# One forward transform in place of two for values and weights in an attention-plus-FFN kernel, with the values' second form made by DMA

## The chip, the core and the metric

The kernel is one program on one core of a Trainium2 chip. The metric is the device time of one execution in microseconds; the number to predict is the median over runs of the changed kernel. The core has five engines that take part here: TensorE (PE in the profile, its weight loads are PEld), VectorE (DVE), ScalarE (ACT), GpSimd (POOL), and SyncE (SP), whose queue issues every DMA of this program. Each engine carries out its own instructions in order, and semaphores tie the engines together.

## The reference, cut to what matters

Sixteen batches of 64 tokens with 512 channels go through two residual blocks. The first is an autocorrelation attention between the normalised x and a context, for every channel on its own; the second is a gated FFN of width 1792 in float16 weights.

```python
# block 1: q = layernorm(x), k = v = ctx, every channel alone, length L = 64
corr = ifft(fft(q) * conj(fft(k))).real
w, idx = top_k(corr, 8)
w = softmax(w)
out = sum over i of w[i] * v[min(idx[i] + pos, L - 1)]
x = x + tanh(g_xattn) * out
# block 2
h = silu(layernorm(x) @ W_gate.T) * (layernorm(x) @ W_up.T)
x = x + tanh(g_ffn) * (h @ W_down.T)
```

## The kernel before, in words

Two batches make a pair (128 partitions), and there are eight pairs, 0 to 7. Fourier transforms are matmuls with constant matrices. Keys, queries, values and weights are transformed with a contraction of 64 rows (one batch), 128 output rows and 512 channels.

For pairs 1 to 7 every float32 operand is split into a float16 high and a float16 low part (steps named `..._hi` on ScalarE and `..._lo` on GpSimd). One transform of a pair is then six matmuls of 64x512 (three products of parts for each of two batches; helper `transform`, L785). A batch's rows are partitions 0 to 63 or 64 to 127, so the two batches use different row halves of the array. Pair 0 is not split and runs in float32 (`transform32`, L793).

The gather with a clamped index is done as a correlation over twice the length, so that values and weights are needed at the even and at the odd frequencies of length 128. Per pair the steps are these:

- `kspec` transforms the context at even frequencies, `kcopy` (two ACT copies, L563) takes the result out of PSUM into `kv_spec`; `vspec` transforms the context at odd frequencies, `vcopy` (two ACT copies, L569) takes that out; `qspec` transforms the queries. All three use PSUM banks 4 and 5, so each waits for the copies of the one before.
- `prod` (DVE, L663) multiplies queries with keys, `p_hi` and `p_lo` split it, `lags` (24 small matmuls, L866 to L868) transforms back to correlations over lags.
- The softmax over the best eight: `max` (L673), `sub` (L681 for all lags and L683 for the best eight), `match` (L696), `exp` (ACT, L585 and L586), `sum` (DVE: the sum L702, the mask L704, the reciprocal L706), `scale` (GpSimd L503; for pair 0 on DVE, L710).
- `w_rows_hi`, `w_rows_lo` split the weights, `w_t` (two transposing DMAs, L450) turns them; for pair 0 `wt` does it on TensorE.
- `wspec:p` transforms the weights at even frequencies, `mix_prod:p` and `mix_prod:p.1` (DVE, L727) multiply by the even spectra; `wspec:p.1` transforms them at odd frequencies into the same PSUM banks 6 and 7, and `mix_prod:p.2`, `:p.3` multiply by the odd spectra. `m_hi` and `m_lo` split the products, `mix` (12 matmuls, L918) transforms back.
- `residual` (DVE, L745, with the statistics L640, L642) adds to x; `rstd2` (GpSimd), `xn`, `x_rows_hi` (ACT), `x_rows_lo` (GpSimd, L522) and `x_t` (two transposing DMAs, L460) make the FFN's input.
- The FFN runs in four parts per pair: `gate`, `up` (L802, 128 or 64 columns a matmul), `tanh` (ACT, L624), `silu` (DVE, L764), `hid` (DVE, L772), `h_hi` (ACT, L631), `h_lo` (GpSimd, L527), `down` (L967), then `out` and `store`.

The order of all steps is written out by hand in one list, `ORDER`. Each engine walks the list and carries out its own part of each step, so the list fixes every engine's order, SP's too. `kspec` of a pair waits until `match` and `sub` of the pair before are done, since banks 4 and 5 hold the correlations too. The attention of later pairs is laid between the FFN parts of earlier ones. `mixed` and `kv_spec` have two buffers each. `WARM_UP` gives the number of matmuls on zeroed data at three places of pair 0 (L815): at the start, before `kspec:1` and before `wt:0`.

Of the kernel before, what the change touches and what calls it, by code (L numbers as in the profile page):

```python
# [112 lines left out]
warm:0 stats1:0 rstd1:0 kspec:0 q_norm:0 qspec:0 kcopy:0 kcopy:0.1 vspec:0 prod:0 stats1:1 k_hi:1 lags:0  # L113
vcopy:0 prod:0.1 rstd1:1 vcopy:0.1 max:0 lags:0.1 warm:0.1 sub:0 k_lo:1 q_norm:1 match:0 exp:0 kspec:1
warm:0.2 q_hi:1 sum:0 q_lo:1 scale:0 kcopy:1 max:0.1 wt:0 kcopy:1.1 sub:0.1 w_hi:0 vspec:1 match:0.1 gates:0
wspec:0 exp:0.1 scales:0 vcopy:1 sum:0.1 wspec:0.1 vcopy:1.1 mix_prod:0 qspec:1 scale:0.1 mix_prod:0.2 wt:0.1
mix:0 prod:1 stats1:2 p_hi:1 mix:0.1 w_hi:0.1 p_lo:1 prod:1.1 wspec:0.2 residual:0 p_hi:1.1 k_hi:2 p_lo:1.1
wspec:0.3 mix_prod:0.1 rstd2:0 lags:1 mix_prod:0.3 max:1 rstd1:2 xn:0 xt:0 sub:1 k_lo:2 mix:0.2 q_norm:2
x_hi:0 match:1 mix:0.3 k_hi:3 q_hi:2 k_lo:3 x_lo:0 exp:1 kspec:2 residual:0.1 q_lo:2 gate:0 kcopy:2 sum:1
rstd2:0.1 up:0 tanh:0 scale:1 kcopy:2.1 silu:0 xn:0.1 vspec:2 w_rows_hi:1 hid:0 gate:0.1 w_t:1 w_rows_lo:1  # L120
stats1:3 vcopy:2 vcopy:2.1 rstd1:3 h_hi:0 qspec:2 xt:0.1 prod:2 h_lo:0 up:0.1 x_hi:0.1 w_t:1.1 p_hi:2 x_lo:0.1
prod:2.1 tanh:0.1 p_lo:2 gate:0.2 stats1:4 p_hi:2.1 q_norm:3 p_lo:2.1 silu:0.1 hid:0.1 wspec:1 rstd1:4
h_hi:0.1 lags:2 mix_prod:1 up:0.2 mix_prod:1.1 m_hi:1 h_lo:0.1 max:2 k_hi:4 m_lo:1 q_hi:3 wspec:1.1 sub:2
m_hi:1.1 gate:0.3 m_lo:1.1 mix_prod:1.2 exp:2 match:2 tanh:0.2 q_lo:3 mix:1 m_hi:1.2 tanh:0.3 m_lo:1.2 sum:2
kspec:3 up:0.3 mix_prod:1.3 kcopy:3 scale:2 silu:0.2 m_hi:1.3 hid:0.2 kcopy:3.1 m_lo:1.3 mix:1.1 w_rows_hi:2
silu:0.3 vspec:3 h_hi:0.2 hid:0.3 w_t:2 w_rows_lo:2 mix:1.2 vcopy:3 residual:1 vcopy:3.1 h_lo:0.2 h_hi:0.3
qspec:3 down:0 rstd2:1 prod:3 w_t:2.1 prod:3.1 p_hi:3 h_lo:0.3 xn:1 down:0.1 x_rows_hi:1 p_lo:3 p_hi:3.1 x_t:1
p_lo:3.1 wspec:2 mix_prod:2 x_rows_lo:1 lags:3 mix_prod:2.1 m_hi:2 down:0.2 max:3 q_norm:4 m_lo:2 x_t:1.1
m_hi:2.1 down:0.3 sub:3 k_lo:4 match:3 exp:3 wspec:2.1 m_lo:2.1 q_hi:4 gate:1 sum:3 mix_prod:2.2 scale:3
kspec:4 mix_prod:2.3 m_hi:2.2 up:1 out:0 m_hi:2.3 m_lo:2.2 w_rows_hi:3 tanh:1 m_lo:2.3 w_t:3 gate:1.1 kcopy:4  # L130
silu:1 kcopy:4.1 w_rows_lo:3 stats1:5 mix:2 hid:1 q_lo:4 mix:2.1 mix:2.2 w_t:3.1 h_hi:1 vspec:4 residual:2
h_lo:1 up:1.1 vcopy:4 vcopy:4.1 rstd2:2 tanh:1.1 qspec:4 k_hi:5 silu:1.1 wspec:3 prod:4 gate:1.2 prod:4.1
p_hi:4 mix_prod:3 p_hi:4.1 p_lo:4 mix_prod:3.1 up:1.2 tanh:1.2 p_lo:4.1 hid:1.1 xn:2 silu:1.2 x_rows_hi:2
k_lo:5 gate:1.3 hid:1.2 h_hi:1.1 x_t:2 lags:4 h_hi:1.2 h_lo:1.1 down:1 tanh:1.3 max:4 m_hi:3 h_lo:1.2 match:4
up:1.3 x_rows_lo:2 down:1.1 rstd1:5 sub:4 x_t:2.1 silu:1.3 exp:4 wspec:3.1 hid:1.3 h_hi:1.3 kspec:5
mix_prod:3.2 q_norm:5 h_lo:1.3 down:1.2 sum:4 kcopy:5 m_lo:3 kcopy:5.1 mix_prod:3.3 m_hi:3.1 scale:4 gate:2
m_lo:3.1 w_rows_hi:4 m_hi:3.2 w_t:4 down:1.3 w_rows_lo:4 tanh:2 up:2 m_hi:3.3 out:1 m_lo:3.2 silu:2 gate:2.1
m_lo:3.3 w_t:4.1 hid:2 stats1:6 h_hi:2 q_hi:5 mix:3 mix:3.1 q_lo:5 mix:3.2 vspec:5 residual:3 h_lo:2 up:2.1
vcopy:5 rstd1:6 vcopy:5.1 tanh:2.1 qspec:5 rstd2:3 wspec:4 prod:5 gate:2.2 silu:2.1 p_hi:5 prod:5.1 p_lo:5
hid:2.1 p_hi:5.1 up:2.2 tanh:2.2 p_lo:5.1 h_hi:2.1 silu:2.2 xn:3 h_lo:2.1 gate:2.3 hid:2.2 x_rows_hi:3 lags:5  # L140
mix_prod:4 x_t:3 tanh:2.3 h_hi:2.2 silu:2.3 up:2.3 mix_prod:4.1 m_hi:4 h_lo:2.2 down:2 hid:2.3 k_hi:6 max:5
m_hi:4.1 k_lo:6 h_hi:2.3 down:2.1 match:5 q_norm:6 x_rows_lo:3 k_hi:7 h_lo:2.3 sub:5 x_t:3.1 down:2.2 m_lo:4
exp:5 m_lo:4.1 wspec:4.1 q_hi:6 kspec:6 mix_prod:4.2 down:2.3 mix_prod:4.3 m_hi:4.2 sum:5 kcopy:6 gate:3
m_lo:4.2 kcopy:6.1 out:2 m_hi:4.3 scale:5 up:3 tanh:3 m_lo:4.3 w_rows_hi:5 silu:3 w_t:5 gate:3.1 w_rows_lo:5
q_lo:6 mix:4 tanh:3.1 mix:4.1 w_t:5.1 silu:3.1 mix:4.2 vspec:6 residual:4 up:3.1 vcopy:6 vcopy:6.1 hid:3
rstd2:4 qspec:6 wspec:5 prod:6 gate:3.2 mix_prod:5 p_hi:6 prod:6.1 xn:4 p_lo:6 mix_prod:5.1 p_hi:6.1 up:3.2
hid:3.1 tanh:3.2 p_lo:6.1 x_rows_hi:4 silu:3.2 h_hi:3 x_t:4 wspec:5.1 h_hi:3.1 h_lo:3 gate:3.3 mix_prod:5.2
x_rows_lo:4 lags:6 hid:3.2 tanh:3.3 m_hi:5 up:3.3 silu:3.3 h_lo:3.1 x_t:4.1 m_hi:5.1 down:3 store:0 h_hi:3.2
m_lo:5 hid:3.3 m_hi:5.2 mix_prod:5.3 down:3.1 max:6 h_lo:3.2 m_hi:5.3 h_hi:3.3 sub:6 h_lo:3.3 gate:4 k_lo:7
match:6 m_lo:5.1 down:3.2 tanh:4 exp:6 m_lo:5.2 up:4 sum:6 m_lo:5.3 stats1:7 scale:6 down:3.3 silu:4 kspec:7  # L150
rstd1:7 out:3 mix:5 hid:4 kcopy:7 mix:5.1 kcopy:7.1 mix:5.2 w_rows_hi:6 vspec:7 residual:5 h_hi:4 w_t:6
gate:4.1 q_norm:7 rstd2:5 up:4.1 tanh:4.1 w_rows_lo:6 vcopy:7 silu:4.1 xn:5 gate:4.2 w_t:6.1 vcopy:7.1 hid:4.1
store:1 q_hi:7 x_rows_hi:5 q_lo:7 up:4.2 tanh:4.2 x_t:5 h_hi:4.1 store:2 silu:4.2 h_lo:4 qspec:7 h_lo:4.1
hid:4.2 wspec:6 prod:7 h_hi:4.2 x_rows_lo:5 gate:4.3 mix_prod:6 p_hi:7 prod:7.1 down:4 m_hi:6 h_lo:4.2 x_t:5.1
mix_prod:6.1 store:3 m_hi:6.1 p_lo:7 up:4.3 p_hi:7.1 tanh:4.3 p_lo:7.1 wspec:6.1 silu:4.3 down:4.1
mix_prod:6.2 m_lo:6 hid:4.3 m_hi:6.2 mix_prod:6.3 h_hi:4.3 m_lo:6.1 lags:7 m_hi:6.3 down:4.2 max:7 h_lo:4.3
m_lo:6.2 match:7 gate:5 m_lo:6.3 sub:7 down:4.3 tanh:5 exp:7 up:5 out:4 sum:7 mix:6 silu:5 scale:7 mix:6.1
hid:5 mix:6.2 gate:5.1 w_rows_hi:7 residual:6 w_t:7 w_rows_lo:7 up:5.1 rstd2:6 tanh:5.1 silu:5.1 xn:6 w_t:7.1
gate:5.2 hid:5.1 x_rows_hi:6 h_hi:5 x_t:6 store:4 h_hi:5.1 h_lo:5 up:5.2 tanh:5.2 silu:5.2 x_rows_lo:6 wspec:7
hid:5.2 h_lo:5.1 x_t:6.1 gate:5.3 mix_prod:7 up:5.3 tanh:5.3 h_hi:5.2 silu:5.3 down:5 mix_prod:7.1 m_hi:7  # L160
m_hi:7.1 m_lo:7 wspec:7.1 h_lo:5.2 down:5.1 mix_prod:7.2 hid:5.3 m_hi:7.2 mix_prod:7.3 gate:6 m_hi:7.3
h_hi:5.3 h_lo:5.3 down:5.2 m_lo:7.1 tanh:6 silu:6 m_lo:7.2 up:6 m_lo:7.3 down:5.3 mix:7 out:5 mix:7.1 mix:7.2
hid:6 gate:6.1 residual:7 h_hi:6 h_lo:6 up:6.1 tanh:6.1 rstd2:7 silu:6.1 xn:7 gate:6.2 hid:6.1 up:6.2 tanh:6.2
x_rows_hi:7 silu:6.2 h_hi:6.1 x_t:7 gate:6.3 hid:6.2 h_lo:6.1 up:6.3 h_hi:6.2 x_rows_lo:7 tanh:6.3 down:6
silu:6.3 hid:6.3 h_lo:6.2 x_t:7.1 h_hi:6.3 store:5 down:6.1 h_lo:6.3 down:6.2 gate:7 down:6.3 tanh:7 up:7
silu:7 out:6 store:6 gate:7.1 hid:7 up:7.1 tanh:7.1 h_hi:7 silu:7.1 h_lo:7 gate:7.2 hid:7.1 up:7.2 tanh:7.2
h_hi:7.1 silu:7.2 h_lo:7.1 gate:7.3 hid:7.2 up:7.3 h_hi:7.2 tanh:7.3 h_lo:7.2 down:7 silu:7.3 hid:7.3 h_hi:7.3
# [20 lines left out]
def on_vector(step, p, n):  # L190
# [809 lines left out]
```

## Time and profile before

| | |
|---|---|
| median of 3 runs | 225.96 us (225.72 to 226.12) |
| the profiled execution's own time | 226.68 us |
| its span, first to last instruction | 224.8 us |
| mean granted TensorE clock | 0.991 of full |
| PE busy | 215.2 us, 96% |
| DVE, POOL, ACT busy | 138.3, 137.7, 111.0 us |

The span is 1.88 us shorter than the profiled execution's own time, and that execution is 0.72 us above the median of the runs. Busy times are of one execution. A matmul's own length in the trace (381 ns for 512 columns) contains the pipeline's fill, so that neighbours overlap; what a group of matmuls costs is read from the chain of work or from the distance between starts.

### The profile page before, as it was taken

To read this page: it belongs to the slowest core of one execution; us is meant where nothing else is said; L and a number is where in the kernel's file an instruction comes from. 1 tells how busy PE (TensorE), PEld (TensorE's weight loads), DVE (VectorE), ACT (ScalarE), POOL (GpSimd) and SP (SyncE) were. 2 spreads that over 40 slices of the span, in tenths; PEclk is the share of its full clock that TensorE was granted. 3 is DMA by queue.
4 is the path that set the end of the run, shared out by engine and by line. 5 is a ranking of instruction groups with operands and counts; after the bars stand their busy time and mean duration, and the time that the engine had idled before them with its cause. 6 is when DMAs were issued, how large, how long until landed. Compare 5 with 4: busy or idle time off the path is not lost.

```text
span 224.8 us, 6753 instructions
## 1 busy us (share of the span) xinstructions
PE 215.2 (96%) x2779; PEld 148.4 (66%) x2779; DVE 138.3 (61%) x407; ACT 111.0 (49%) x208; POOL 137.7 (61%) x165
## 2 busy tenths in 40 slices
...
GB/s 152 335 434 425 388 140 50 4 3 47 47 4 51 0 50 0 50 3 23 28 25 26 23 73 3 23 143 70 4 26 93 26 0 3 25 73 50 0 3 47
DMA packets 19918, 16.69 MB, mean 74 GB/s; under 512 B 15920, under 2 KB 16304, under 8 KB 19504
## 3 DMA queue, kind: packets, MB, share of 16 engines
...
## 4 chain that ended last, share of the span: by engine, by line
PE 86%; DVE 6%; DMA 2%; issue 2%; POOL 1%; ACT 1%; SPq 0%; DVEq 0%; ACTq 0%
PE psum L802 44%; PE psum L967 20%; PE psum L785 10%; PE psum L918 4%; PE psum L903 2%; DMA ctx_sb<-ctx 2%; DVE probs L696 1%; DVE raw_stats L640 1%; PE psum L793 1%; PE psum L885 1%; PE psum L866 1%; ACT xn L537 1%; DVE x_sb L745 1%; PE psum L867 1%; PE psum L868 1%
## 5 line engine op out<-in xcount | busy, mean ns | idle before, releaser
L802 PE MATMUL psum<-xt_hi,wg 128*128 128x128 f16 (+1 forms) x504 | 54.0, 213 | 0.0
L802 PE MATMUL psum<-xt_hi,wu 128*128 128x128 f16 (+1 forms) x504 | 53.9, 213 | 0.0
L802 PE MATMUL psum<-xt_lo,wg 128*128 128x128 f16 (+1 forms) x504 | 53.9, 213 | 0.0
L802 PE MATMUL psum<-xt_lo,wu 128*128 128x128 f16 (+1 forms) x504 | 53.8, 213 | 0.0
L527 POOL TENSOR_TENSOR hid_lo<-hid,hid_hi 128x512 f16<-128x512 f32 (+2 forms) x32 | 33.0, 1037 | 29.0 <-ACT hid_hi L631 29.0
L802 PEld LDWEIGHTS psum<-xt_hi,wg 128*128 128x128 f16 x504 | 44.8, 98 | 6.2 <-issue 5.5
L802 PEld LDWEIGHTS psum<-xt_hi,wu 128*128 128x128 f16 x504 | 44.9, 98 | 3.0 <-issue 2.1
L802 PEld LDWEIGHTS psum<-xt_lo,wu 128*128 128x128 f16 x504 | 45.0, 98 | 0.8
L802 PEld LDWEIGHTS psum<-xt_lo,wg 128*128 128x128 f16 x504 | 45.1, 98 | 0.7
L967 PE MATMUL psum<-wd,hid_hi 128*128 128x512 f16 x112 | 42.5, 379 | 0.1
L967 PE MATMUL psum<-wd,hid_lo 128*128 128x512 f16 x112 | 42.4, 379 | 0.0
L764 DVE SCALAR_TENSOR_TENSOR act<-act,psum 128x512 f32<-128x512 f32 (+2 forms) x32 | 19.7, 616 | 32.7 <-ACT act L624 32.4
L513 POOL TENSOR_TENSOR mixed_lo<-mixed,mixed_hi 128x512 f16<-128x512 f32 x28 | 32.6, 1177 | 4.4 <-ACT mixed_hi L602 4.4
L624 ACT ACTIVATE act<-psum 128x512 f32<-128x512 f32 (+2 forms) x32 | 17.2, 539 | 35.2 <-PE psum L802 35.2
L727 DVE SCALAR_TENSOR_TENSOR mixed<-psum,kv_spec 128x512 f32<-128x512 f32 x32 | 21.3, 680 | 10.0 <-PE psum L785 10.0
L631 ACT ACTIVATE hid_hi<-hid 128x512 f16<-128x512 f32 (+2 forms) x32 | 18.0, 570 | 14.8 <-DVE hid L772 14.7
L772 DVE TENSOR_TENSOR hid<-act,psum 128x512 f32<-128x512 f32 (+2 forms) x32 | 19.8, 618 | 8.4 <-PE psum L802 5.9
L498 POOL TENSOR_TENSOR prod_lo<-prod,prod_hi 128x512 f16<-128x512 f32 x14 | 16.1, 1158 | 11.3 <-ACT prod_hi L575 11.1
L602 ACT ACTIVATE mixed_hi<-mixed 128x512 f16<-128x512 f32 x28 | 17.4, 625 | 10.6 <-DVE mixed L727 10.5
L967 PEld LDWEIGHTS psum<-wd,hid_hi 128*128 128x128 f16 x112 | 11.0, 98 | 12.9 <-issue 1.8
L967 PEld LDWEIGHTS psum<-wd,hid_lo 128*128 128x128 f16 x112 | 11.0, 98 | 10.6
L663 DVE TENSOR_TENSOR prod<-psum,kv_spec 128x512 f32<-128x512 f32 x16 | 10.8, 685 | 8.7 <-PE psum L785 4.6
...
## 6 DMA issues: line engine op xcount, KB each, us to landing
out<-x_sb SPq DMA_DIRECT2D x8, 256.0 KB, 2.3
...
x_sb<-x SPq DMA_DIRECT2D x4, 256.0 KB, 5.2
ctx_sb<-ctx SPq DMA_DIRECT2D x4, 256.0 KB, 5.1
...
```

What stands on the lines that cost most here:

```text
L498: nc.gpsimd.tensor_tensor(prod_lo[:, e, n, :], prod[:, e, n, :], prod_hi[:, e, n, :], ALU.subtract).then_inc(split_sems["p_lo", False], 1)
L513: nc.gpsimd.tensor_tensor(mixed_lo[:, e, n, :], mixed[:, e, n, :], mixed_hi[:, e, n, :], ALU.subtract).then_inc(split_sems["m_lo", False], 1)
L527: nc.gpsimd.tensor_tensor(hid_lo[:, e, first:end, tok], hid32[:, n % 2, 0:ffn_cols(p, n)].rearrange("p (a t) -> p a t", a=end - first), hi ...
L602: nc.scalar.activation(mixed_hi[:, e, n, :], mixed[:, e, n, :], ACT.Copy).then_inc(mixed_high, 1)
L624: nc.scalar.activation(act32[:, n % 2, 0:cols], psum[:, gate_bank(p, n), 0:cols], ACT.Tanh, scale=0.5).then_inc(tanh_done, 1)
L631: nc.scalar.activation(hid_hi[:, e, first:end, tok], hid32[:, n % 2, 0:ffn_cols(p, n)].rearrange("p (a t) -> p a t", a=end - first), ACT.C ...
L727: nc.vector.scalar_tensor_tensor(mixed[:, e, n, :], psum[:, w_bank(p, m, b), :], MIX_UP, kv_spec[:, e, n, :], ALU.mult, ALU.mult).then_inc ...
L764: nc.vector.scalar_tensor_tensor(a, a, 1.0, psum[:, gate_bank(p, n), 0:cols], ALU.add, ALU.mult).then_inc(silu_done, 1)
L772: nc.vector.tensor_tensor(hid32[:, n % 2, 0:cols], act32[:, n % 2, 0:cols], psum[:, up_bank(p, n), 0:cols], ALU.mult).then_inc(hid_done, 1)
L785: last = nc.tensor.matmul(psum[:, banks[b], :], consts[rows(b), forward(name, part)], data[rows(b), :], start=data is high and part == 0, ...
L802: last = nc.tensor.matmul(psum[:, bank, a * n:(a + 1) * n], w[:, k, m * P:(m + 1) * P], xt[:, e, k, tok], start=(k == 0 and part == 0), st ...
L967: last = nc.tensor.matmul(psum[:, down_bank(p), :], hid[:, e, m, :], wd[:, m, :], start=(m == 0 and part == 0), stop=(m == MT - 1 and part ...
```

## The change

- For pairs 1 to 7 there is one transform of the context, with the matrix `values`: 64 columns of even frequencies and 64 of odd ones. Keys and values come out of the same result. `vspec` remains for pair 0 alone.
- `vcopy` of a pair is one ACT copy of 128 x 1024 (two banks); `kcopy` is two ACT copies of 64 x 1024, which write the even half into the upper and the lower 64 partitions of `k_spec`. `qspec` waits for all three.
- The values' second form (real and imaginary parts exchanged) is not transformed: the new step `turn` issues five DMAs on SP's queue, four from `v_spec` to `v_turned` in SBUF (31 or 32 partitions x 4 KB each) and one of two context rows (4 KB) from HBM.
- There is one transform of the weights per pair (matrix `weights`), and all four `mix_prod` follow it. The second pair of them waits for the five DMAs.
- `mixed` has one buffer in place of two, so `mix_prod` of a pair waits for `m_lo` of the pair before.
- The softmax's steps are cut finer: `sub` and `sub8`, `exp` and `exp8`, `total` (sum and reciprocal) and `mask`, each with its semaphore, with the same instructions.
- The two last loads (context and x of pairs 4 to 7, 1 MB each) are issued behind `turn:1` and no longer at the start.
- `WARM_UP` goes from ((12, 4), (3, 7), (2, 7)) to ((12, 4), (0, 7), (11, 7)), that is 12, 0 and 11 matmuls. `ORDER` is another list. Pair 0 keeps its float32 arithmetic.

```diff
-WARM_UP = ((12, 4), (3, 7), (2, 7))
+WARM_UP = ((12, 4), (0, 7), (11, 7))
...
-    kv_spec = sb("kv_spec", [P, 2, 4, D])
+    v_spec = sb("v_spec", [P, 2, 2, D])
+    v_turned = sb("v_turned", [P, 2, 2, D])
+    k_spec = sb("k_spec", [P, 2, 2, D])
...
-    mixed = sb("mixed", [P, 2, 4, D])
+    mixed = sb("mixed", [P, 4, D])
...
+                if step == "turn":
+                    sp.wait_ge(v_copied, copies(p))
+                    if p > 2:
+                        sp.wait_ge(mixed_done, 4 * p - 4)
+                    for to, first, count in ((1, 33, 31), (32, 0, 32), (64, 96, 32), (96, 64, 32)):
+                        sp.dma_start(v_turned[to:to + count, e, :, :], v_spec[first:first + count, e, :, :])\
+                          .then_inc(v_moved[e], 16)
+                    sp.dma_start(v_turned[0:1, e, :, :], last_rows[p:p + 1, :, :]).then_inc(v_moved[e], 16)
+                    if p == 1:
+                        load(ctx_sb, cv, 4, PAIRS, ctx_loaded[4])
+                        load(x_sb, xv, 4, PAIRS, x_loaded[4])
...
+                if step == "vcopy" and p > 0:
+                    act.wait_ge(k_spectra, p + 1)
...
+                    nc.scalar.activation(v_spec[:, e, :, :], psum[:, k_bank(p, 0):k_bank(p, 1) + 1, :], ACT.Copy,
                                          scale=SPEC).then_inc(v_copied, 1)
+                if step == "kcopy" and p > 0:
...
+                    nc.scalar.activation(k_spec[rows(n), e, :, :], psum[0:L, k_bank(p, 0):k_bank(p, 1) + 1, :], ACT.Copy,
+                                         scale=SPEC).then_inc(k_copied, 1)
...
+                if step == "mix_prod" and p > 0:
+                    m, b = n // 2, n % 2
+                    dve.wait_ge(w_spectra, nth("wspec", p))
+                    if m == 0:
+                        dve.wait_ge(v_copied, copies(p))
+                    else:
+                        dve.wait_ge(v_moved[e], nth_turned(p))
+                    if p == 1:
+                        dve.wait_ge(mix_done, last_of("residual", 0))
+                    else:
+                        dve.wait_ge(*split_count("m_lo", p - 1, n))
+                    nc.vector.scalar_tensor_tensor(mixed[:, n, :], psum[:, w_bank(p, m, b), :], MIX_UP,
+                                                   (v_spec, v_turned)[m][:, e, b, :], ALU.mult, ALU.mult)\
+                      .then_inc(mixed_done, 1)
...
-                        pe.wait_ge(k_copied, 2 * p + 2)
-                        last = transform(banks, "odd_v", k_hi[:, e, :], k_lo[:, e, :])
...
-                    transform([w_bank(p, n, b) for b in range(2)], ("even", "odd")[n], w_hi[:, e, :], w_lo[:, e, :])\
+                    transform([w_bank(p, 0, b) for b in range(2)], "weights", w_hi[:, e, :], w_lo[:, e, :])\
```

The parts of the new `ORDER` that the prediction speaks of (each "..." leaves steps out):

```
vcopy:0 prod:0.1 lags:0 ... max:0 sub:0 q_hi:1 kspec:1 warm:0.2 sub8:0
max:0.1 exp:0 q_lo:1 exp8:0 kcopy:1 match:0 total:0 vcopy:1 sub:0.1 mask:0 sub8:0.1 scale:0
...
mix:1.2 ... down:0 ... down:0.1 ... wspec:2 ... lags:3 ... down:0.2 max:3 k_lo:4 down:0.3
x_t:1.1 sub:3 match:3 exp:3 rstd1:5 q_norm:4 m_hi:2 sub8:3 kspec:4 mix_prod:2.1 exp8:3
m_lo:2 gate:1
...
q_lo:4 mix:2.1 vcopy:4 mix:2.2 w_rows_lo:3 up:1.1 h_hi:1 residual:2 k_hi:5 rstd1:6 w_t:3.1 tanh:1.1 qspec:4
rstd2:2 turn:3 gate:1.2 prod:4 prod:4.1 p_hi:4 silu:1.1 p_hi:4.1 p_lo:4 up:1.2 tanh:1.2 xn:2 h_lo:1 silu:1.2
hid:1.1 x_rows_hi:2 wspec:3 p_lo:4.1 h_hi:1.1 x_t:2 gate:1.3 mix_prod:3 x_rows_lo:2 hid:1.2 lags:4 tanh:1.3
```

## Rows read from the trace of the kernel before

**Rows 1.** Busy time by stage, us (and instructions): PE, PEld, DVE, ACT, POOL, clock, DMA.
```profile
0.00:30.30 30.30, 25.74 (x122) 10.42 (x123) 21.76 (x84) 15.76 (x31) 12.58 (x24) 0.94 0.92 345
30.30:62.60 32.30, 30.41 (x597) 20.25 (x596) 24.48 (x81) 21.77 (x41) 27.43 (x33) 1.00 0.14 29
62.60:215.00 152.40, 152.40 (x2031) 114.66 (x2030) 90.42 (x241) 72.52 (x135) 95.91 (x107) 1.00 0.16 33
```

**Rows 2.** Groups of PE's instructions: busy us, mean ns; the transforms of the context.
```profile
L785 PE MATMUL psum<-k_hi,consts 64*128 64x512 f16 x56 | 10.8, 381 | 0.7 <-DVE probs L696 0.5
```

**Rows 3.** Chain of work, 70 to 75 us: start, us, what.
```profile
70.35 0.75 PE psum L785 x6
...
73.00 1.40 PE psum L785 x12
```

**Rows 4.** PE in order of time: first matmuls of gate:1 and of gate:2.
```profile
62.55 0.23 PE L802 MATMUL psum<-xt_hi,wg 128*128 128x128 f16 x1
...
87.09 0.22 PE L802 MATMUL psum<-xt_hi,wg 128*128 128x128 f16 x1
```

**Rows 5.** PE in order of time: lags:3, with the idle time before it.
```profile
58.41 0.19 PE L866 MATMUL psum<-consts,prod_hi 128*128 128x64 f16 x1 [0.48 <-POOL prod_lo L498]
```

**Rows 6.** Chain of work, pair 0's first softmax half: start, us, what.
```profile
10.67 0.55 DVE top L673 x4
...
11.23 0.42 DVE expo L681
11.66 0.91 DVE expo L683
...
14.11 1.18 DVE probs L710
```

**Rows 7.** DVE in order of time: pair 0's second L683.
```profile
16.19 0.18 DVE L683 TENSOR_TENSOR expo<-top 128x32 f32<-128x32 f32 x1
```

**Rows 8.** Busy time by stage inside pair 0's work, the columns of group 1.
```profile
12.00:15.30 3.30, 1.90 (x11) 0.41 (x9) 3.16 (x14) 2.29 (x6) 1.79 (x2) 1.00 0.99 421
15.30:19.00 3.70, 3.66 (x20) 1.58 (x20) 3.67 (x22) 2.07 (x6) 0.00 (x0) 1.00 0.98 417
...
27.00:29.50 2.50, 2.50 (x6) 0.27 (x4) 2.16 (x18) 1.86 (x5) 1.91 (x3) 0.50 1.05 387
```

**Rows 9.** Groups of ACT's instructions, shapes apart: busy us, mean ns, idle before.
```profile
L569 ACT ACTIVATE kv_spec<-psum 128x512 f32<-128x512 f32 x16 | 8.8, 593 | 4.9 <-PE psum L785 4.7
...
L624 ACT ACTIVATE act<-psum 128x256 f32<-128x256 f32 x7 | 2.6, 374 | 4.5 <-PE psum L802 4.5
```

**Rows 10.** DMA issues: count, KB each, median us to landing.
```profile
out<-x_sb SPq DMA_DIRECT2D x8, 256.0 KB, 2.3
...
ctx_sb<-ctx SPq DMA_DIRECT2D x4, 256.0 KB, 5.1
...
xt_lo<-xn_lo SPq DMA_TRANSPOSE x7, 2.5
```

**Rows 11.** SP's queue in order of time: start, us to issue.
```profile
9.16 0.67 SPq L437 DMA_DIRECT2D wd<-w_down  x1
...
69.10 1.19 SPq L450 DMA_TRANSPOSE w_lo<-w_lo_rows  x1
78.32 1.19 SPq L460 DMA_TRANSPOSE xt_hi<-xn_hi  x1
82.30 1.19 SPq L460 DMA_TRANSPOSE xt_lo<-xn_lo  x1
```

**Rows 12.** POOL in order of time, from p_lo:4 to x_rows_lo:2.
```profile
75.23 2.29 POOL L498 TENSOR_TENSOR prod_lo<-prod,prod_hi 128x512 f16<-128x512 f32 x2 [1.81 <-ACT prod_hi L575]
77.47 1.16 POOL L490 TENSOR_TENSOR k_lo<-ctx_sb,k_hi 128x512 f16<-128x512 f32 x1
78.89 2.27 POOL L527 TENSOR_TENSOR hid_lo<-hid,hid_hi 128x512 f16<-128x512 f32 x2 [0.25 <-ACT hid_hi L631]
81.12 1.15 POOL L522 TENSOR_TENSOR xn_lo<-xn,xn_hi 128x512 f16<-128x512 f32 x1
```

More of the change, by code:

```diff
@@ L95, in parts @@
         return high, (m - high).astype(np.float16)
-    for n, m in enumerate((even_kv, even, odd_v, odd)):
+    for n, m in enumerate((query, values, weights)):
         for part, v in enumerate(parts(m)):
@@ L112 @@
 ORDER = """
[L113 to L167, printed above, removed]
@@ L168 @@
-h_lo:7.3 down:7.1 down:7.2 down:7.3 out:7 store:7
+warm:0 stats1:0 rstd1:0 kspec:0 q_norm:0 kcopy:0 qspec:0 kcopy:0.1 vspec:0 stats1:1 prod:0 k_hi:1 rstd1:1
+vcopy:0 prod:0.1 lags:0 vcopy:0.1 k_lo:1 lags:0.1 warm:0.1 q_norm:1 max:0 sub:0 q_hi:1 kspec:1 warm:0.2 sub8:0
+max:0.1 exp:0 q_lo:1 exp8:0 kcopy:1 match:0 total:0 vcopy:1 sub:0.1 mask:0 sub8:0.1 scale:0 kcopy:1.1 stats1:2
+wt:0 w_hi:0 qspec:1 match:0.1 rstd1:2 exp:0.1 wspec:0 gates:0 prod:1 exp8:0.1 prod:1.1 p_hi:1 wspec:0.1
+mix_prod:0 k_hi:2 p_lo:1 q_norm:2 mix_prod:0.2 mix:0 mask:0.1 p_hi:1.1 total:0.1 mix:0.1 q_hi:2 scale:0.1
@@ new lines @@
+p_lo:1.1 scales:0 residual:0 k_lo:2 lags:1 k_hi:3 wt:0.1 max:1 w_hi:0.1 rstd2:0 wspec:0.2 sub:1 q_lo:2 xn:0
+wspec:0.3 match:1 exp:1 k_lo:3 xt:0 mix_prod:0.1 kspec:2 sub8:1 mix:0.2 mix_prod:0.3 exp8:1 x_hi:0 mask:1
+kcopy:2 mix:0.3 turn:1 x_lo:0 total:1 vcopy:2 gate:0 residual:0.1 scale:1 kcopy:2.1 stats1:3 rstd2:0.1 qspec:2
+tanh:0 w_rows_hi:1 up:0 prod:2 w_t:1 w_rows_lo:1 prod:2.1 p_hi:2 silu:0 xn:0.1 p_lo:2 gate:0.1 p_hi:2.1
+stats1:4 p_lo:2.1 xt:0.1 w_t:1.1 hid:0 tanh:0.1 up:0.1 x_hi:0.1 silu:0.1 rstd1:3 h_hi:0 x_lo:0.1 turn:2 lags:2
```

223 lines of the change are left out of this document (146 added, 77 removed).

## The prediction

> **What bounds the kernel now.** I read the busy time by stage first. The reader is to see three stretches [rows 1]. From 62.6 us, where the FFN of pair 1 begins, to 215 us PE is busy for 152.40 of 152.40 us, while DVE has 90.4, POOL 95.9 and ACT 72.5 us of work: TensorE alone sets the time there, and a matmul less is time less. From 30.3 to 62.6 us PE has 30.41 of 32.30 us, but POOL has 27.43: two engines are nearly full. Up to 30.3 us (pair 0) PE has 25.74 us, DVE 21.76, and the chain of work runs over DVE's softmax [rows 6].
>
> Then I read what a transform costs. The group of PE's instructions gives a matmul 381 ns [rows 2]; six would be 2.3 us. That is the wrong number: it holds the pipeline's fill, and the two row halves run beside each other. The chain of work gives 0.75 us for six matmuls that stand alone and 1.40 us for twelve in a row [rows 3], so a transform is worth 0.75 us alone and 0.65 us where it stands beside another one.
>
> **The change part by part.**
>
> *Fewer transforms.* Seven `vspec` and seven second `wspec` go, 84 matmuls. Which of the fourteen lie in the full stretch follows from the order: `gate:1` began at 62.55 us [rows 4], and `vspec:4` to `vspec:7` and `wspec:3.1` to `wspec:7.1` stand behind it, nine. Two of them (`wspec:3.1`, `wspec:4.1`) stood beside a `kspec`: 7 x 0.75 + 2 x 0.65 = 6.55 us, call it 6.6. The other five (`vspec:1`, 2 and 3, `wspec:1.1`, `wspec:2.1`) would be 5 x 0.75 = 3.75 us if PE were the bound there too. `vspec:1` lies in pair 0's stretch, under DVE's softmax, and is worth nothing. The other four lie where POOL has 27.43 of 32.30 us; `lags:3` even waited 0.48 us for `p_lo` [rows 5]. And `kspec:4` moves from behind `gate:1` to before it. It needs `match:3`, which follows `lags:3`, `max` and `sub`: DVE's pieces of a whole pair are twice those of half a pair (0.55 and 0.42 us for `max` and `sub` [rows 6]), and only two parts of `down` and nothing else cover them, now that `wspec:2.1` is gone. So I take 1.7 of the 3.75 us, between 0 and 3.75.
>
> *Pair 0's order.* Before, `scale:0` came after one half's chain alone. Now `max:0.1`, `sub:0.1` and `sub8:0.1` stand ahead of it: 0.55 + 0.42 + 0.2 to 0.9 us [rows 6, 7], 1.2 to 1.9 us later for `wt:0`. The second half gains most of that back, since its pieces are done already, and `stats1:1` leaves the place between the two `prod`. Behind it, `mix_prod:0.1` and `mix_prod:0.3` now stand after `max:1`, `sub:1` and `match:1`. Net, I take 0.7 us lost up to the first `gate`; bounds 0 and 1.5. The eleven warming matmuls lie where PE waits for `scale:0` anyway: PE was busy 1.90 of 3.30 us from 12.0 to 15.3 us [rows 8]. From 27.0 to 29.5 us the granted clock was 0.50, that is 1.2 GHz, behind a time in which PE had waited [rows 8]. The new order leaves such waits in the same place, so I take that loss as it is; at full clock these 2.5 us would be some 1.25 us, a bound on the other side.
>
> *Copies on ACT.* Before, four copies of 512 columns per pair, 593 ns each; 256 columns take 374 ns [rows 9], so 1,024 columns come to 593 + 2 x 219 = 1.03 us. Three of them are 3.1 us a pair against 4 x 0.59 = 2.4 us, 0.7 us more, 5 us in all. ACT has 72.5 of 152.4 us in the full stretch [rows 1], which hides it. `qspec` waits for all three behind `kspec`; in the new order `mix`, parts of `down` and `up` or more stand between. Cost nothing; were the cover gone, up to 3.1 us a pair.
>
> *`turn` on DMA and on SP's queue.* The trace has no copy from SBUF to SBUF. The nearest rows are a 256 KB store in 2.3 us and a 256 KB load in 5.1 us [rows 10]; the four pieces are 128 KB each, so 2.3 to 5.1 us to land behind the last issue. An issue takes 0.67 us [rows 11], a transpose's 1.19; five are 3.4 to 6.0 us. So `v_turned` is there 6 to 11 us after `turn` begins. I take the lower end, since the DMA share in the full stretch is 0.16 [rows 1]. Who waits: `mix_prod:p.2`. For pair 3 it stands between `x_t:2` and `x_t:2.1` in the order, at 78.32 and 82.30 us before, and SP is free from 70.3 us [rows 11]: 8 to 12 us. What is queued behind it on SP: for pairs 3 to 5 the next `x_t`, for pair 6 `w_t:6.1`. SP stood idle from 69.10 + 1.19 to 78.32 us before `x_t:2` [rows 11], 8 us, which hides 3.4 to 6.0. Nothing, then.
>
> By a rule of the Trainium skill ("SBUF — State Buffer", Door 1: The DMA port swizzle) partitions 0 to 31 reach only eight of the sixteen DMA ports of SBUF, so each of these copies of 32 partitions would run at no more than half the rate of a full one. No row here shows it. By the rule the landing time would be the upper one, and the sum would stay as it is as long as that fits into the 8 to 12 us above.
>
> *Moved loads.* The last two loads are issued behind `turn:1`. In the rows the DMA share is full up to 29.5 us [rows 8] with the weights ahead of them, so the queue is still fed when they come, and `k_hi:4`, the first to need them, stands just before `lags:3`, which began at 58.41 us [rows 5]. Nothing.
>
> *One buffer of `mixed`, finer softmax.* `m_lo` of the pair before is a whole pair back: nothing. The finer steps are the same instructions. Their price depends on what stands beside them: L683 took 0.91 us with GpSimd at work and 0.18 us in a stretch in which GpSimd did nothing [rows 6 to 8]. This agrees with the Trainium skill ("SBUF — State Buffer", the part on the shared pair), by which a VectorE instruction with two SBUF inputs and a GpSimd instruction lock each other out. By that rule, with GpSimd denser after the change, the seven masks and seven `sub8` would take up to 0.7 us longer each, 10 us of DVE in all; DVE has 62 us of room in the full stretch, so the sum stays.
>
> *New waits in the full stretch.* The cover between the helpers' chain and the FFN shrinks. `x_t:2.1` was issued at 82.30 us and lands 2.5 us later [rows 10, 11], 84.8 us; `gate:2` began at 87.09 [rows 4]: 2.3 us of room, and two transforms (1.4 us) leave it. But `x_rows_lo:2` also moves: it stood behind two `p_lo`, one `k_lo` and two `h_lo` [rows 12], now behind two `p_lo` and one `h_lo`, two times 1.15 us earlier. I take 0.5 us for all pairs together; bounds 0 and 3.3 (half of 6.6).
>
> **Sum.** -6.6 - 1.7 + 0.7 + 0.5 = -7.1 us. The profiled execution's 226.68 us become 219.6; the median of the runs is 0.72 us below that execution, so 225.96 - 7.1 = 218.9 us.
>
> **The rivals.**
>
> *A, everything counts.* PE bounds the start too, and the stretch at half clock goes: 6.55 + 3.75 = 10.3 us, up to 11.5 with the clock: 214.5 to 215.7 us. For it: PE is 94% busy from 30.3 to 62.6 us, and the order is new as a whole. Against it: POOL's 27.43 us there [rows 1].
>
> *B, the helpers become the bound.* With 6.6 us less, POOL's 95.9 us lie in some 146 us, 66%, but the work comes in bursts, and `gate` of each pair waits for a chain with 2.3 us of room [rows 4, 11]. PE then waits 0.5 us or so in each of six pairs, and the start gives nothing: -6.6 + 0.7 + 3.3 = -2.6, 223.4 us; halfway from my forecast, 221.2. For it: the waits at 58.4 us [rows 5]. Against it: the chain of POOL's steps is shortened as well [rows 12].
>
> *C, SP's queue holds up `x_t` (slower).* SP is in order. If `turn` had to wait for something late, or an issue took as long as it takes to land, the five would hold the queue for 5 x 2.3 = 11.5 us. That is 3.5 us more than SP's idle time of 8 us; less the 2.3 us of room, `gate` comes 1.2 us late, and with the 5.1 us a piece of the slow row 5 x 5.1 - 8 - 2.3 = 15 us late. It decides from 10.3 us a `turn` on, and makes the kernel slower from about 1.5 us a pair over that for pairs 3 to 7. With 3 us for each of five pairs: -7.1 + 15 = +7.9, 233.9 us. Against it: these issues return in 0.67 to 1.19 us, their data land 2.3 to 5.1 us later [rows 10, 11].
>
> *D, no change.* Would need the same at about 1.4 us a pair; nothing in the rows speaks for it.
>
> **How the numbers follow.** My forecast, 0.62; A 0.12; B 0.20; C 0.04; D 0.02. The forecast's own range is 217.3 to 220.9: the start's term between 0 and 3.75 with the loss of pair 0 against it. The range for 8 in 10 goes to A's upper end, 215.6, and into B, 222.5. Under 0.2% (0.45 us) a measurement cannot tell from no change. Faster: forecast, A and B, 0.94; same 0.02; slower 0.04.
>
> **What the profile after would show.** PE's L785-like groups have 126 matmuls instead of 210, and PE's busy time is about 10 us less (1.3 us come back as warming matmuls). The full stretch has PE at 100% still, if B is wrong; waits for `x_t`'s DMAs before `gate` would show B or C. ACT's copies in pairs 1 to 7 sum to about 21 us. The five `turn` issues stand in SP's idle time; a wait of `mixed` for a DMA would make my reading of `turn` wrong. The first `gate` matmul starts at 30.3 to 31.8 us. Gate:1 starting before 61 us would mean that the start gave more than I allow; after 63.5 us, that it gave nothing.

## The result: 1.7% slower, and the profile after

The changed kernel takes 229.88 us (median of 4 runs, 228.90 to 231.27), the kernel before on the same chip 226.04 us (225.72 to 226.48). The ratio is 1.017, 95% interval 1.011 to 1.024. The forecast was 218.9 us, 11 us too low, with the wrong sign. The profiled execution took 230.77 us, with a span of 228.7 us.

Busy time by stage, the columns and stretches of [rows 1]:

```profile
0.00:30.30 30.30, 25.76 (x133) 10.94 (x134) 21.12 (x87) 19.70 (x33) 13.68 (x25) 0.94 0.90 314
30.30:62.60 32.30, 28.10 (x557) 20.82 (x554) 21.57 (x65) 17.82 (x30) 23.29 (x30) 0.89 0.55 84
62.60:215.00 152.40, 144.14 (x1915) 109.65 (x1914) 90.22 (x253) 77.13 (x134) 98.64 (x108) 1.00 0.35 51
```

In the stretch in which TensorE was busy for 152.40 of 152.40 us it now is for 144.14: 8.3 us of idle time have come into a stretch that had none. The DMA share has gone from 0.16 to 0.35 there. Seven `turn` of 0.52 MB are not much in bytes, so the share (the time that packets are in the engines) says that packets wait there. In the second stretch the clock is 0.89 in place of 1.00. The wait list of PE says for what it waited (us in total, times, longest):

```profile
PE psum L869 <- issue: 4.7, 2, 2.8
PE psum L886 <- issue: 2.6, 1, 2.6
PE psum L869 <- DVE probs L765: 1.8, 2, 1.2
PE psum L886 <- DMA xt_lo<-xn_lo: 1.7, 1, 1.7
```

L869 is `transform` (L785 before), L886 `gate` and `up` (L802 before). "Issue" is a wait for which the view names nobody. The two of L869 stand right before `wspec:4` and `wspec:6`, whose operands are brought by transposing DMAs; the one of 2.6 us of L886 lies before 40.2 us, at the start. These DMAs' median times from issue to landing stand beside it (before, `w_hi` took 2.5, `w_lo` 3.2, `xt_hi` 2.4 and `xt_lo` 2.5 us):

```profile
w_hi<-w_hi_rows SPq DMA_TRANSPOSE x7, 2.5
w_lo<-w_lo_rows SPq DMA_TRANSPOSE x7, 4.6
xt_hi<-xn_hi SPq DMA_TRANSPOSE x7, 4.1
xt_lo<-xn_lo SPq DMA_TRANSPOSE x7, 3.3
```

`w_hi` is mostly issued ahead of a `turn` and keeps its 2.5 us. The others are often issued right behind one: the eight transposes that follow `turn:3` to `turn:6` directly land 5.2 to 7.4 us after their issue, the same ones in experiment 2's kernel without `turn` after 2.4 to 4.3. The median of `xt_lo` alone says nothing, since it is 3.6 us in that kernel. Now SP's queue around two of them (start, us to issue); L497 is the four copies from SBUF to SBUF, L499 the two context rows:

```profile
95.08 1.19 SPq L511 DMA_TRANSPOSE w_hi<-w_hi_rows  x1
96.37 3.42 SPq L497 DMA_DIRECT2D v_turned<-v_spec  x4
99.83 0.65 SPq L499 DMA_DIRECT2D v_turned<-ctx  x1
...
101.84 1.69 SPq L511 DMA_TRANSPOSE w_lo<-w_lo_rows  x1
...
127.80 2.94 SPq L497 DMA_DIRECT2D v_turned<-v_spec  x4
130.78 0.65 SPq L499 DMA_DIRECT2D v_turned<-ctx  x1
131.53 1.22 SPq L521 DMA_TRANSPOSE xt_hi<-xn_hi  x1
...
133.54 1.71 SPq L521 DMA_TRANSPOSE xt_lo<-xn_lo  x1
```

The five issues of `turn:4` take 4.1 us, those of the others 3.6 to 5.3, inside the 3.4 to 6.0 us that the prediction allowed. They are not what holds the queue up. What follows them is, in the chain of work:

```profile
106.06 1.96 issue
...
133.54 6.01 DMA xt_lo<-xn_lo
139.64 1.95 PE psum L886 x32
...
150.09 2.78 issue
```

The transpose at 133.54 lands 6.0 us later, and `gate:4` starts at 139.64 with it.

The second half of the products waits too. DVE stood 2.3 us before `mix_prod:3.2` (at 84.96 us) and 2.4 us before `mix_prod:5.2`; with 30 and 1 rows (experiment 1) neither wait is there:

```profile
84.96 0.69 DVE L810 SCALAR_TENSOR_TENSOR mixed<-psum,v_turned 128x512 f32<-128x512 f32 x1 [2.32 <-issue]
...
136.71 1.29 DVE L810 SCALAR_TENSOR_TENSOR mixed<-psum,v_turned 128x512 f32<-128x512 f32 x2 [2.42 <-DMA v_turned<-ctx]
```

For the first the view names nobody; the last packet of `turn:3` ended at 84.29 us. On the chain of work it leads to a hole of PE of 0.6 us before `kspec:5`.

The start has its own loss. `gate:1` began at 66.36 us, 3.8 us later than before [rows 4]:

```profile
66.36 0.23 PE L886 MATMUL psum<-xt_hi,wg 128*128 128x128 f16 x1
```

DVE waited for the moved load of x, and behind it PE stood still from 38 to 40 us and then ran at the lower clock, 0.50, for 6 us (row of DVE in order of time, then windows):

```profile
39.98 0.69 DVE L711 BATCH_NORM_STATS2 raw_stats<-x_sb 128x6 f32<-128x512 f32 x1 [5.32 <-DMA x_sb<-x]
```

```profile
38.00:40.00 2.00, 0.00 (x0) 0.00 (x0) 0.02 (x1) 0.00 (x0) 0.18 (x1) 0.81 0.18 46
40.00:46.00 6.00, 5.77 (x103) 5.57 (x105) 5.44 (x30) 1.89 (x4) 3.12 (x5) 0.50 0.41 100
```

And in SP's queue, the last line is the issue of that load, which took 5.87 us where the one before it took 0.41:

```profile
13.63 2.65 SPq L497 DMA_DIRECT2D v_turned<-v_spec  x4
16.32 0.94 SPq L499 DMA_DIRECT2D v_turned<-ctx  x1
17.31 0.41 SPq L469 DMA_DIRECT2D ctx_sb<-ctx  x1
17.77 5.87 SPq L469 DMA_DIRECT2D x_sb<-x  x1
```

So in both places what is queued behind a `turn` is late. The trace's DMA packets tell how. Of `turn:4` they are 4 KB each. Counted per half microsecond, they come at up to 20 from 99 to 102.5 us, and from 102.5 us at 2 to 5 until the last ends at 104.97; the tail of the load of x, packets of 2 KB, comes at 5 to 7 per half microsecond from 35.5 to 39.5 us, with a packet taking 84 ns. 6 x 84 ns is 0.5 us: one after the other without a pause, as from a single DMA engine (the trace doesn't name the engines). Of the five pieces one has an odd form, 31 rows (1 to 31 of `v_turned`); the other three have 32.

**Theory K.** The copy of 31 rows is carried by one DMA engine, all 31 x 4 KB, since 31 can't be divided among several. Each engine works through its queue in order, so every transfer issued behind it waits for that one engine. The Trainium skill ("DMA: Bandwidth & Descriptors", Why a DMA increments its semaphore by 16 and not by 1) has this as a rule: a DMA is shared by the largest number of engines up to 16 that divides the slowest dimension, so 100 partitions go to ten engines and 127 to one. By it 31 rows would go to one engine and 30 to fifteen.

The rivals to be told apart were these: the port rule of the prediction (each copy of 32 partitions is slow); the number of issues on SP's queue; the moved loads; the new order itself.

### The profile page after: what moved, and what is told of

Same layout as the page of the kernel before. It is cut to its first block, busy times and chain, and to the rows that moved or that the text cites. A ratio compares the mean times of both kernels' runs of the same rounds, so it can differ in the third digit from the quotient of the medians.

```text
span 228.7 us, 6635 instructions
## 1 busy us (share of the span) xinstructions
PE 208.5 (91%) x2701; PEld 148.3 (65%) x2701; DVE 135.9 (59%) x407; ACT 117.1 (51%) x201; POOL 138.6 (61%) x165
## 4 chain that ended last, share of the span: by engine, by line
PE 63%; issue 9%; POOL 8%; DVE 7%; SPq 5%; DMA 4%; ACT 2%; DVEq 0%; ACTq 0%; POOLq 0%
PE psum L886 34%; PE psum L1043 13%; PE psum L869 5%; PE psum L994 3%; PE psum L899 3%; SPq L497 3%; POOL mixed_lo L575 3%; DMA xt_lo<-xn_lo 3%; DMA v_turned<-ctx 2%; PE psum L979 1%; SPq L511 1%; POOL prod_lo L559 1%; POOL q_lo L555 1%; POOL w_lo_rows L571 1%; POOL k_lo L551 1%
## 5 line engine op out<-in xcount | busy, mean ns | idle before, releaser
L886 PE MATMUL psum<-xt_hi,wg 128*128 128x128 f16 (+1 forms) x504 | 55.5, 216 | 1.7 <-DMA xt_lo<-xn_lo 1.7
L886 PE MATMUL psum<-xt_lo,wu 128*128 128x128 f16 (+1 forms) x504 | 54.3, 214 | 2.6 <-issue 2.6
L886 PE MATMUL psum<-xt_lo,wg 128*128 128x128 f16 (+1 forms) x504 | 55.4, 216 | 0.0
L886 PE MATMUL psum<-xt_hi,wu 128*128 128x128 f16 (+1 forms) x504 | 54.4, 214 | 0.0
L886 PEld LDWEIGHTS psum<-xt_hi,wg 128*128 128x128 f16 x504 | 46.3, 100 | 6.6 <-issue 3.8
L886 PEld LDWEIGHTS psum<-xt_hi,wu 128*128 128x128 f16 x504 | 45.1, 98 | 4.1 <-issue 3.3
L886 PEld LDWEIGHTS psum<-xt_lo,wu 128*128 128x128 f16 x504 | 45.4, 98 | 3.4 <-issue 2.7
L886 PEld LDWEIGHTS psum<-xt_lo,wg 128*128 128x128 f16 x504 | 46.5, 100 | 0.6
L711 DVE BATCH_NORM_STATS2 raw_stats<-x_sb 128x6 f32<-128x512 f32 (+1 forms) x17 | 11.7, 690 | 10.9 <-DMA x_sb<-x 10.6
L535 POOL TENSOR_SCALAR var_eps<-mean_var 128x1 f32<-128x1 f32 (+1 forms) x17 | 3.8, 223 | 21.7 <-DVE mean_var L713 21.1
```

The lines of the kernel that those rows point to most:

```text
L711: nc.vector.bn_stats(raw_stats[tok, n, :], x_sb[tok, p, :]).then_inc(raw_done, 1)
L886: last = nc.tensor.matmul(psum[:, bank, a * n:(a + 1) * n], w[:, k, m * P:(m + 1) * P], xt[:, e, k, tok], start=(k == 0 and part == 0), st ...
```

## The experiments

The ratios are to the kernel before on the same chip, which took 225.89 us beside experiments 1 and 2, 226.11 beside 4 to 6, and 226.14 beside 3 and 7.

**1. The copy of 31 rows in two, 30 and 1.** One issue more, the same bytes:

```diff
-for to, first, count in ((1, 33, 31), (32, 0, 32), (64, 96, 32), (96, 64, 32)):
+for to, first, count in ((1, 33, 30), (31, 63, 1), (32, 0, 32), (64, 96, 32), (96, 64, 32)):
```

> The copy of 31 rows is issued as one of 30 rows and one of 1 row, six DMAs a pair in place of five, the same bytes. Theory K (the 31 rows are all carried by one DMA engine, whose last packets come about 4 us after the others', and transposes and loads that are queued on that engine wait for them): the holes of PE before wspec:4, gate:4 and wspec:6 (1.96, 1.7 and 2.8 us) and DVE's wait of 5.3 us for x_sb go, and the time falls from 229.9 to 219 to 221 us. Theory Q (SP's in-order queue, 3.6 to 5.3 us of issuing a pair, is what delays the transposes): one more issue, 229.9 or up to 231. Theory L (the two loads issued behind turn:1 are what delays the start): 229.9, no change.

Measured: 220.15 us (219.29 to 220.49), ratio 0.974, 0.972 to 0.976. One more DMA per pair makes the kernel 9.7 us faster than the changed one and 5.7 us faster than the one before. The last two stages of busy time, and the transposes:

```profile
30.30:62.60 32.30, 29.39 (x583) 20.38 (x583) 26.04 (x88) 20.30 (x36) 26.20 (x34) 0.98 0.32 85
62.60:215.00 152.40, 151.28 (x2002) 115.41 (x1998) 87.71 (x234) 76.93 (x134) 98.83 (x107) 1.00 0.25 50
```

```profile
w_lo<-w_lo_rows SPq DMA_TRANSPOSE x7, 2.5
xt_hi<-xn_hi SPq DMA_TRANSPOSE x7, 2.4
xt_lo<-xn_lo SPq DMA_TRANSPOSE x7, 2.7
```

PE's idle time in the full stretch is 1.1 us in place of 8.3, the medians of the transposes are at 2.4 to 2.7 us, and the moved load is issued in half a microsecond:

```profile
18.22 0.50 SPq L469 DMA_DIRECT2D x_sb<-x  x1
```

The number of issues is out as a cause: this kernel has more of them.

**2. Parts of `turn` left out.** Three kernels in which all four products read `v_spec`, and `v_turned` is used by nothing: without the copy of 31 rows; with it and the context rows alone; and without any DMA of `turn`.

```diff
-for to, first, count in ((1, 33, 31), (32, 0, 32), (64, 96, 32), (96, 64, 32)):
+for to, first, count in ((32, 0, 32), (64, 96, 32), (96, 64, 32)):    # or ((1, 33, 31),):   or no DMA
```

> The copy of 31 rows is left out, three copies of 32 rows and the one from HBM remain; the second pair of products reads v_spec, so the values' second form is left out of the result. Theory K: as without any copy, 218 to 220 us. Theory Q: one issue of five less, a fifth of the loss, 228 us. Theory B (the bytes of the copies): a quarter of the loss less, 227 us.

> The three copies of 32 rows are left out, the one of 31 rows and the one from HBM remain; the second pair of products reads v_spec, so the values' second form is left out of the result. Theory K: still slow, 227 to 230 us. Theory Q and theory B: two issues of five and a quarter of the bytes are left, 221 to 223 us.

> All five DMAs of turn are left out and nothing waits for them; the second pair of products reads v_spec, so the values' second form is left out of the result. The loads keep their place behind vcopy:1. If the copies' DMAs are the whole loss against my sum, 217.5 to 220 us, by all of K, Q and B. If the new order or the copies on ACT cost as well, 222 us or more. Theory L: the start keeps its wait for x_sb, 223 us.

Measured: 219.17 us (218.42 to 219.89) without the copy of 31 rows, 222.82 (222.15 to 224.84) with it and without the three of 32, 218.61 (218.30 to 218.90) without any. The three copies of 32 rows and the two context rows together cost 0.6 us, so the port rule is out as the cause. The copy of 31 rows costs 4.2 us by itself. The new order is out too: without `turn` it is 7.3 us faster than the kernel before.

The costs don't add up: 0.6 and 4.2 us apart, 11.3 us together. The profiles show where the 11.3 us lie. Against the kernel without `turn`, the changed one starts `gate:1` 4.7 us later (66.36 against 61.70) and has holes of PE of 0.6, 2.0, 1.7 and 2.8 us behind it, before `kspec:5`, `wspec:4`, `gate:4` and `wspec:6`: 11.8 of the 12.2 us between the two spans (228.7 and 216.5). The kernel with the one copy starts `gate:1` 0.6 us later (62.30) and has two holes, 2.5 and 1.1 us, with 3.4 us at a clock of 0.50 behind the first. If these cost 1.7 us, that makes 5.9 of its 6.0 us. The three issues fewer let the transposes behind it into the queues 1.8 us sooner after the start of `turn:4`. That this and the missing 32-row copies explain its smaller holes fits the traces and was not measured.

**3. The disputed cost by itself: 30 rows in place of 31.** The kernel with the one copy, a row shorter; the row left out is not copied.

```diff
-for to, first, count in ((1, 33, 31),):
+for to, first, count in ((1, 33, 30),):
```

> The disputed cost by itself: as the kernel with the 31-row copy alone (222.8 us; the other copies of turn left out but for the context rows, all four products read v_spec), but with 30 rows, so 3% fewer bytes in a copy that fifteen engines can share; the one row left out is not copied at all. Theory K (31 rows go to one DMA engine and hold up what is queued behind them): the 4.2 us that the 31-row copy cost over the kernel with no copies (218.6 us) go, 218.4 to 219.4 us, and no hole before wspec:4, gate:3, gate:4. Rival (a copy from SBUF to SBUF, its two issues or its wait costs this by its presence or its bytes): 222 to 223 us.

Measured: 218.61 us (218.40 to 219.48), ratio 0.968, 0.965 to 0.970. A copy with 3% fewer bytes costs nothing where the longer one cost 4.2 us. SP's queue around `turn:4`, first with 31 rows, then with 30:

```profile
92.95 0.61 SPq L497 DMA_DIRECT2D v_turned<-v_spec  x1
...
96.58 1.43 SPq L511 DMA_TRANSPOSE w_lo<-w_lo_rows  x1
```

```profile
91.89 0.86 SPq L497 DMA_DIRECT2D v_turned<-v_spec  x1
...
95.76 1.19 SPq L511 DMA_TRANSPOSE w_lo<-w_lo_rows  x1
```

The issue itself is the first sign: 0.61 us for 31 rows, 0.86 us for 30, which is shorter for the longer copy (medians of the seven 0.64 and 0.88 us). The trace's packets are the second. Each line: the 4 KB packets of this copy, first start and last end in us:

```
31 rows: 31 packets, 94.2 to 100.7: 6.4 us
30 rows: 30 packets, 93.4 to 94.2:  0.8 us
```

With 31 rows the starts of two packets lie at least 155 ns apart and never more than two packets are open at once; with 30 rows up to 15 are. The trace names no engine, but this is what one engine and fifteen would look like. The transposes' packets of 256 bytes take 18 ns in the median. Beside the copy of 31 rows, 18 of them are open for 1.8 to 3.0 us each, and all 18 end between 100.92 and 100.97 us, 0.3 us behind the copy's last packet (100.65). So the transposes wait for the slow copy, and since 18 are open at once where the slow copy has at most two, engines without a share in it seem to be held as well. Why they are is not shown.

**4. 29 and 2 rows in place of 30 and 1.** The same number of issues and bytes as experiment 1; 29 is prime too.

```diff
-for to, first, count in ((1, 33, 30), (31, 63, 1), ...
+for to, first, count in ((1, 33, 29), (30, 62, 2), ...
```

> The copy of 31 rows is issued as 29 rows and 2 rows, six DMAs as with 30 and 1, the same bytes, nearly the same lengths. Theory K with the rule that the number of engines is the largest number up to 16 that divides the rows: 29 is prime, one engine carries 29 rows, so it stays slow, 227 to 230 us. Theory S (a shorter or divided copy is all that helps): 220 us as with 30 and 1.

Measured: 228.62 us (226.66 to 230.81), ratio 1.010, 1.007 to 1.012, against 220.15 us for 30 and 1. Where the boundary lies between two copies of the same total is worth 8.5 us. With "a copy of about 30 rows is slow" this can't be explained, with the divisors it can. An odd count that has divisors, 27 say, was not run, so that "31 and 29 are odd" is told from "31 and 29 have no divisor up to 16" only by the 15 packets that are open at once with 30 rows.

**5. The loads back at the start,** with the copy of 31 rows, and with 30 and 1.

```diff
+            load(ctx_sb, cv, 4, PAIRS, ctx_loaded[4])        # behind the other loads at the start
+            load(x_sb, xv, 4, PAIRS, x_loaded[4])
...
-                    if p == 1:
-                        load(ctx_sb, cv, 4, PAIRS, ctx_loaded[4])
-                        load(x_sb, xv, 4, PAIRS, x_loaded[4])
```

> The changed kernel with its copy of 31 rows, but the two loads of pairs 4 to 7 issued at the start again, ahead of turn:1. Theory K (one DMA engine carries the 31 rows and whatever is queued behind them on it is late): x_sb no longer comes late at 40 us, gate:1 begins near 62.3 us and not at 66.4, and 3.8 to 4.1 us of the loss go; the holes before wspec:4, gate:4 and wspec:6 stay: 225 to 226.5 us. Theory L (the moved loads alone are the start's loss) gives the same; that they would be harmless behind a divided copy was seen with 30 + 1 rows. If moving them does nothing, 229.9, both are wrong on the start.

> 30 + 1 rows and the loads at the start. With no engine late the place of the loads decides nothing: 219.5 to 220.5 us, the same as 30 + 1 alone (220.15).

Measured: 228.70 us (226.90 to 230.22) with 31 rows. That is a miss by the median: in the profiled execution the loss at the start is gone (`gate:1` at 61.91 us, 4.4 us earlier), but the median is only 1.2 us lower, and the four executions lie 3.3 us apart. That execution, 226.90 us, had a mean clock of 0.992; the changed kernel's two executions at 0.992 took 228.9 and 229.0 us, so at the same clock the place of the loads is worth an estimated 2 us. The idle time in the full stretch stays (144.71 us busy of 152.40). So the moved loads explain part of the start and none of the rest. With 30 and 1: 219.47 us (218.81 to 220.63), ratio 0.972, 0.969 to 0.976. It is 0.7 us below experiment 1, and the two ranges overlap; this is the lowest median of a version that computes everything.

**6. `turn` behind the transposes.** With 30 and 1 rows, `turn:4` stands behind `w_t:4.1` and `turn:6` behind `w_t:6.1` in `ORDER`.

```diff
-... p_hi:5 turn:4 prod:5.1 ... w_t:4.1
+... p_hi:5 prod:5.1 ... w_t:4.1 turn:4
```

> 30 + 1 rows, and turn:4 and turn:6 stand behind w_t:4.1 and w_t:6.1 in SP's order. What is left between 30 + 1 rows (220.15) and no copy at all (218.61) is 1.5 us, with a hole of 1.0 us before wspec:4, which waits for w_t:4.1 behind turn:4. If SP's order is that rest, the hole goes and the time is 218.8 to 219.5 us; if v_turned then comes late for mix_prod:4.2, 220 us or more.

Measured: 219.86 us (219.72 to 220.29), within the spread of experiment 1. The hole of 1.0 us before `wspec:4` went, and one of 1.4 us before `gate:3` and one of 0.3 us later came: `x_t` now waits behind `turn` instead. With the slow copy gone, there is no more to be had from the place of `turn` in these two pairs.

**7. The copy of 31 rows issued last.**

```diff
-for to, first, count in ((1, 33, 31), (32, 0, 32), (64, 96, 32), (96, 64, 32)):
+for to, first, count in ((32, 0, 32), (64, 96, 32), (96, 64, 32), (1, 33, 31)):
```

> The changed kernel with the 31-row copy issued behind the three of 32 rows in place of ahead of them; same bytes, same number of issues. Theory K as it stands (one engine carries 31 x 4 KB, and the whole turn and all that is queued behind it wait for that engine): the copies of 32 rows no longer wait, but the product that waits for all five and the transposes behind them do, so 228 to 231 us, the start lost too (gate:1 behind 65 us). Rival L (the loss is that the copies of 32 rows stand behind the slow one on its engine and fill SP's queue, so that SP's own issues stall): 221 to 225 us.

Measured: 234.85 us (230.97 to 237.69, four executions 7 us apart; the ratio, 1.028, 1.019 to 1.038, leaves out the two longest). Rival L (the copies of 32 rows behind the slow one are the loss) is out: it wanted 221 to 225 us, and the shortest execution took 230.97. K has the sign, and its 228 to 231 us were too low by the median. That this order is slower than the changed kernel is not sure: by its ratio, without the two longest, it is at 232.5 us, and the two ratios' intervals overlap. The trace shows one reason for a longer time. Issued last, the slow copy also starts last, and its last packet ended at 107.64 us, 9.9 us behind the start of its `turn`, against 104.97 - 96.37 = 8.6 us with it first. The clock is a second one: behind the holes of PE it was at 0.50 in two stretches of 3.4 us (from 110.7 and from 144.8 us) that the changed kernel's profile has not, while the one near 42 us is 3.4 us shorter. How much each is worth was not measured.

## Why the prediction was wrong

**The step that failed** is that `turn` costs "Nothing, then", and in it the price "the four pieces are 128 KB each, so 2.3 to 5.1 us to land behind the last issue". The rows behind it [rows 10] are transfers of 128 partitions. I scaled by bytes, kept the number of engines that share a transfer without saying so, and never looked at the counts in `((1, 33, 31), ...)`. The one copy of 31 rows ran for 6.4 us where 30 rows took 0.8, one packet after the other. Then I asked who waits for `v_turned` and who waits for SP, but not who is queued behind `turn` in the DMA engines. The transposes right behind a `turn` landed after 5.2 to 7.4 us, and PE stood for 2.0, 1.7 and 2.8 us before `wspec:4`, `gate:4` and `wspec:6`.

The landing of the whole `turn` was within the range and at its upper end: the last packet of `turn:4` ended 4.5 us behind its last issue, and `mix_prod:3.2` began 9.7 us after `turn:3`, inside the 6 to 11 us. I had taken the lower end and a cover of 8 to 12 us. The cover was 7.4 us at pair 3 and 6.5 at pair 5, so the product did wait, which the prediction had named as the sign that its reading of `turn` is wrong.

**Rival C** named the right victims (`x_t`, then `gate`) and the right sign, with the wrong place: not SP's queue, whose five issues took 3.6 to 5.3 us, but the DMA engines behind it. My argument against it ("these issues return in 0.67 to 1.19 us") was true for most issues and didn't bear on that. Its condition, a `turn` that occupies a queue for 10.3 us, was nearly met in the engines: 8.6 us.

**"Moved loads. Nothing"** failed for the same reason. The moved loads stood behind the slow copy of `turn:1`, whose packets went on to 34.3 us (29.9 with 30 and 1 rows): the statistics on x started at 39.98 us, `gate:1` lost 3.8 us, part of it through the lower clock from 40 to 46 us. With 30 and 1 rows in front of them, moving them cost 0.7 us at most.

**The rest of the sum held,** which experiment 2 without `turn` shows: -7.3 us against -7.1. Its `gate:1` began at 61.70 us, and from there to the end it took 154.8 us against 162.3 before. 7.5 us less, of which 0.75 belong to `kspec:4`, moved ahead of `gate:1`: 6.7 us, with the new waits in it, against -6.6 + 0.5 = -6.1. Of the new waits for which I had 0.5 us none came: PE was busy without a pause to its last matmul at 213.3 us, and the 1.8 us that are missing in the stretch to 215 us lie behind that, since this kernel ends at 216.5 us:

```profile
62.60:205.00 142.40, 142.40 (x1927) 110.07 (x1925) 85.44 (x230) 75.06 (x130) 96.46 (x104) 1.00 0.18 35
205.00:215.00 10.00, 8.23 (x68) 4.67 (x65) 2.28 (x4) 1.32 (x3) 1.83 (x2) 1.00 0.01 4
```

So -6.6 stands against a measured -6.7, and the 0.5 was too much.

The start gave 0.85 us by `gate:1`'s start (61.70 against 62.55), and 1.6 us with `kspec:4` counted in; I had 1.7 - 0.7 = 1.0. The terms read from the two profiles add up to 8.3 us, 1.0 more than the medians show: 0.7 of it is the profiled execution of before, which was that much above its median. So the agreement of -7.3 with -7.1 is in part luck: the start gave 0.6 us more than I had, the waits cost 0.5 us less, and the 1.0 us between profiles and medians hides both. ACT's copies of 1,024 columns were forecast at 1.03 us:

```profile
L645 ACT ACTIVATE k_spec<-psum 64x1024 f32<-64x1024 f32 x14 | 14.2, 1013 | 4.9 <-PE psum L869 4.7
...
L637 ACT ACTIVATE v_spec<-psum 128x1024 f32<-128x1024 f32 x7 | 7.1, 1016 | 0.1
```

PE has 126 of the matmuls as forecast. Its busy time fell by 6.7 us in the changed kernel and by 9.0 in the one without `turn`, of 10 forecast. The first `gate` started at 29.94 us, ahead of the 30.3 to 31.8 forecast; before it was 30.27, so of the 0.7 us that I gave pair 0's order nothing shows in this execution (0.3 us without `turn`, 30.57).

**The forecast's own range,** 217.3 to 220.9, doesn't follow from its bounds: with the start between 0 and 3.75, pair 0 between 0 and 1.5 and 0.5 for the waits they give 216.1 to 221.4 us. The result is far outside either.

**The port rule of the Trainium skill** was weighed in the prediction and decided nothing here: the three copies of 32 partitions cost 0.6 us together with the context rows. The rule that would have given the sign is the one that Theory K draws on, which I had not applied to the row counts of the diff.

**What stays open:** why the slow copy costs 4.2 us by itself but 10.7 us beside the copies of 32 rows (229.88 against 219.17), how it can hold engines that have no share in it, and why a kernel's executions lie 2.4 to 6.7 us apart with the slow copy and within 1.9 us without it. The clock is a part of the last: the changed kernel took 228.9 and 229.0 us at a mean clock of 0.992, 230.8 and 231.3 at 0.978 and 0.976, and the profile at 0.978 shows 6.8 us at 0.50 (from 39.3 us on) behind a hole of PE.
